# Two PSUM banks re-shared, the masked q copies on ScalarE, and new orders of issue in a fused attention, feed-forward and routing kernel

## What is computed

```python
q = sigmoid(x @ Wq + bq); k = sigmoid(x @ Wk + bk); v = x @ Wv + bv     # per head
sink_in = n / sum((q + e) * (cumsum(k) + e));  src_out = n / sum((k + e) * (cumsum(q) + e))
cons_sink = sum((q + e) * (cumsum(k * src_out) + e)) / n
cons_src  = exp(clip(sum((k + e) * (cumsum(q * sink_in) + e)) / n, -1, 1))
qs = q * sink_in / n;  vs = v * cons_src / cumsum(cons_src) * n
attn = (qs @ cumsum(k^T vs)) * sigmoid(cons_sink) @ Wo + bo
h  = layernorm(x + attn) * g1 + be1
h2 = layernorm(h + gelu(h @ W1 + b1) @ W2 + b2) * g2 + be2              # 256 -> 1024 -> 256
r  = layernorm(x + h2)
e  = argmax(r @ router_w)                                               # one of 8 experts
out = layernorm(r + relu(r @ fc[e])**2 @ pj[e])                         # 256 -> 1024 -> 256
```

## Time and profile before

| | us |
|---|---|
| median of 3 runs | 819.72 (818.33 to 820.4) |
| the profiled execution | 821.92 |
| its span, first to last instruction | 819.8 |
| PE busy in it | 782.9 (95%) |
| DVE busy | 558.9 (68%) |
| POOL busy | 368.1 (45%) |
| ACT busy | 311.6 (38%) |

### The profile page before, as it was taken

The page is one execution under the profiler, slowest core; times in us unless marked ns, Lnnn a source line. Parts: engine busy times, 40 slices in busy tenths (PEclk is TensorE's granted clock), DMA queues, the critical chain, the costliest instruction groups (busy, mean ns, idle before and its releaser), DMA issues.

```text
span 819.8 us, 18747 instructions
## 1 busy us (share of the span) xinstructions
PE 782.9 (95%) x6828; PEld 597.2 (73%) x6828; DVE 558.9 (68%) x1209; ACT 311.6 (38%) x571; POOL 368.1 (45%) x563
## 2 busy tenths in 40 slices
PE   7888999999999999999999999999999999999994
PEld 3455687687777777777867867788987778777762
DVE  7788677799889889888889885574663433433332
ACT  2323413533533543443443434343114444333442
POOL 8210613245556356356257275475334433334434
PEclk9998999999999999999999999999999999999998
DMA  8999999100100100100000000894569898888850
GB/s 242 280 315 305 306 290 285 57 2 2 52 21 8 53 21 7 53 15 15 28 14 14 28 21 19 302 354 168 190 220 400 332 345 314 314 309 296 296 194 13
DMA packets 75193, 133.22 MB, mean 162 GB/s; under 512 B 5725, under 2 KB 54111, under 8 KB 75104
## 3 DMA queue, kind: packets, MB, share of 16 engines
q1 hardware_dynamic: 71936, 123.57, 46.2%
q0 software_dynamic: 3168, 8.46, 2.8%
HBM read 89.35 MB, written 42.93 MB: 161 GB/s over the span
## 4 chain that ended last, share of the span: by engine, by line
PE 79%; DVE 9%; POOL 5%; issue 3%; ACT 1%; DMA 1%; POOLq 0%; DVEq 0%; ACTq 0%
PE bank L958 11%; PE bank L993 11%; PE bank L845 7%; PE bank L857 7%; PE bank L653 4%; PE bank L877 4%; PE bank L1005 4%; PE bank L973 4%; PE bank L888 4%; PE bank L769 3%; PE bank L662 3%; PE bank L807 3%; PE bank L823 3%; DVE sm L1583 2%; POOL rstd L1311 1%
## 5 line engine op out<-in xcount | busy, mean ns | idle before, releaser
L1308 POOL TENSOR_SCALAR vare<-mv 128x1 f32<-128x1 f32 x96 | 24.1, 251 | 202.8 <-DVE mv L1590 198.4
L958 PE MATMUL bank<-xsT,fc 128*128 128x128 f32 x800 | 94.1, 276 | 0.5 <-issue 0.5
L958 PEld LDWEIGHTS bank<-xsT,fc 128*128 128x128 f32 x800 | 91.5, 192 | 3.4 <-issue 3.2
L1583 DVE TENSOR_TENSOR sm<-bank,upto 128x512 f32<-128x512 f32 x128 | 79.3, 681 | 17.3 <-PE bank L769 17.2
L993 PE MATMUL bank<-pj,act 128*128 x336 | 76.2, 380 | 0.5 <-issue 0.5
L845 PE MATMUL bank<-n1T,w1s 128*128 128x256 f32 x256 | 69.9, 396 | 1.8 <-ACT n1T L1113 1.8
L1169 ACT ACTIVATE relu<-bank 128x512 f32<-128x512 f32 x68 | 39.9, 595 | 77.0 <-PE bank L958 49.1
L877 PE MATMUL bank<-n1T,w1s 128*128 128x256 f32 x256 | 67.7, 387 | 1.5 <-ACT hT L1135 0.8
L993 PEld LDWEIGHTS bank<-pj,act 128*128 128x128 f32 x336 | 62.2, 190 | 8.3 <-issue 0.8
L888 PE MATMUL bank<-w2s,hT 128*128 128x256 f32 x256 | 67.3, 385 | 0.0
L857 PE MATMUL bank<-w2s,hT 128*128 128x256 f32 x256 | 66.1, 386 | 0.6 <-ACT hT L1118 0.6
(11 more groups left out here) (267 smaller groups left out, 1672.3 us busy)
## 6 DMA issues: line engine op xcount, KB each, us to landing
routed_rows<-empty SPq DMA_DIRECT2D x64, 520.0 KB, 9.6
fc<-in_fc SPq DMA_DIRECT2D x31, 1024.0 KB, 7.2
up_unit<-in_fc SPq DMA_DIRECT2D x24, 1024.0 KB, 8.1
pj<-in_pj SPq DMA_DIRECT2D x8, 1024.0 KB, 12.4
xrow<-in_fc SPq DMA_DIRECT2D x6, 1024.0 KB, 6.8
x<-in_x SPq DMA_DIRECT2D x8, 512.0 KB, 4.1
xT<-in_xT SPq DMA_DIRECT2D x7, 512.0 KB, 5.1
xs<-routed_rows SPq DMA_DIRECT2D x25, 130.0 KB, 5.7
```

Of the source, the lines that this page charges most:

```text
L958: last = nc.tensor.matmul(h_bank[n][:, chunk(f)], fc[:, at, k, chunk(4 * n + f)], xsT[:, k, :], start=(k == 0), stop=(k == KT - 1))
L1583: nc.vector.tensor_tensor(sm[:, n], BANK4[n][:].rearrange("p (h t) -> p h t", h=4), upto[:].unsqueeze(1).broadcast_to([P, 4, P]), ALU.mult ...
```

## The change

1. **Banks.** Both halves of the feed-forward sum in `po0`, one after the other: `down` of the rest waits until `b_half` has read the half (`r2` to 2), `down` of the next half until `b_add` has read the rest (`r2` to 4). `po1` takes the attention output (columns 0 to 255) and the state update (from column 256).
2. **Waits.** `p_pairs`, `a_share1` and `p_share2` no longer wait for `summed` and `r1`. The update inside `p_mix` waits for `summed` and `r1` of the chunk before, and `p_out` for `summed` of its own chunk.
3. **Copies.** All four `qm` copies of a group are made by ACT in its step `p_share2`; POOL's `p_split` is gone.
4. **First wait.** `t_xb` waits for a semaphore of its own, `bo_in`, in place of all nine transfers behind `tables_in`.
5. **Orders.** All lists are new.

```diff
             load_x(0)
-            for tile, src in ((bo, bo_d), (g1, g1_d), (be1, be1_d), (b2, b2_d), (g2, g2_d), (be2, be2_d)):
+            load_rows_of(bo, bo_d, bo_in)
+            for tile, src in ((g1, g1_d), (be1, be1_d), (b2, b2_d), (g2, g2_d), (be2, be2_d)):
                 load_rows_of(tile, src, tables_in)
...
             def share1(g, half, _):
                 ev["cz"].wait(pe, g, 1)
-                ev["summed"].wait(pe, g - 1, 2)
-                ev["r1"].wait(pe, g - 1, 2)
...
             def pairs(g, half, c):
...
-                ev["summed"].wait(pe, g, c)
-                ev["r1"].wait(pe, g, c)
                 ev["sm"].wait(pe, g, 4 * c)
...
             def mix(g, half, c):
...
                 last.then_inc(S["av"], 1)
+                ev["summed"].wait(pe, g, c)
+                ev["r1"].wait(pe, g, c)
                 for m in range(KT):
                     for j in range(HPT // 2):
                         at = m * P + 32 * j
-                        last = nc.tensor.matmul(ps0[32 * j:32 * j + 32, 32 * m:32 * m + 32],
+                        last = nc.tensor.matmul(po1[32 * j:32 * j + 32, STATE + 32 * m:STATE + 32 * m + 32],
...
             def attn_out(g, half, c):
                 ev["xatc"].wait(pe, g, c + 1)
-                ev["sm"].wait(pe, g, 4 * c + 3)
+                ev["summed"].wait(pe, g, c + 1)
                 for m in range(KT):
-                    last = nc.tensor.matmul(pa[:, 0:D], xat[:, c % 2, m, :], wo[:, m, :],
+                    last = nc.tensor.matmul(po1[:, 0:D], xat[:, c % 2, m, :], wo[:, m, :],
...
             def half_down(g, half, f):
...
                 elif f == 0:
-                    ev["r2"].wait(pe, g - 1, NC // 2)
+                    ev["r2"].wait(pe, g - 1, NC)
...
             def down_ffn(g, half, f):
                 ev["gelu"].wait(pe, g, f + 1)
                 if f == 0:
-                    ev["r2"].wait(pe, g - 1, NC)
-                    if g == 0:
-                        ev["v"].wait(pe, 1, 4)
+                    ev["r2"].wait(pe, g, NC // 2)
                 for c in range(NC // 2, NC):
-                    last = nc.tensor.matmul((po0, po1)[c // 2][:, (c % 2) * D:(c % 2) * D + D],
+                    last = nc.tensor.matmul(po0[:, (c % 2) * D:(c % 2) * D + D],
...
-                    if g == 0 and m == KT - 1:
-                        nc.scalar.activation(qm[:, 1, m], qs[:, m], ACT.Copy, scale=parity[:, 1:2])\
-                            .then_inc(S["qm1"], 1)
+                    nc.scalar.activation(qm[:, 1, m], qs[:, m], ACT.Copy, scale=parity[:, 1:2])\
+                        .then_inc(S["qm1"], 1)
...
-            def split_q(g, half, _):
-                for m in range(KT - 1 if g == 0 else KT):
-                    ev["qp"].wait(pool, g, m + 1)
-                    ev["s"].wait(pool, g - 1, 4 * NC)
-                    apart(pool)
-                    nc.gpsimd.tensor_scalar(qm[:, 1, m], qs[:, m], parity[:, 1:2], None, ALU.mult)\
-                        .then_inc(S["qm1"], 1)
...
             def first_xb(g, half, _):
                 dve.wait_ge(x_in[0], 16)
-                dve.wait_ge(tables_in, 16 * 9)
+                dve.wait_ge(bo_in, 16)
...
             def mix(g, half, c):
                 ev["upd"].wait(dve, g, c + 1)
-                own = ps0[:, 0:KT * 2 * DH].rearrange("p (m n) -> p m n", m=KT)
+                own = po1[:, STATE:STATE + KT * 2 * DH].rearrange("p (m n) -> p m n", m=KT)
...
-            def add_h(g, chunks, bank_of):
+            def add_h(g, chunks):
+                if g == 0:
+                    ev["qp"].wait(dve, 1, KT)
...
```

174 lines of the change are left out of this document (82 added, 92 removed), and 8 rows, old and new, of tables (DVE_LAST, POOL_LAST).

## The result

The change made the kernel slower: 824.66 us median (823.28 to 827.42, 8 runs) against 819.66 (816.02 to 823.71, 8 runs), ratio 1.0061 with an interval of 1.0036 to 1.0085. The forecast was 815.5. (Ratios are of times, this kernel over before; an interval that holds 1 shows no difference.)

A forecast was written before the change was run, and what follows sets the result against it. PE was taken to bound the kernel, busy 782.9 of 819.8 us. Start -4.2, periods +0.6 and end -0.6 gave -4.2 us: 815.5 against the median of 819.72; range, to hold 8 in 10, 812.0 to 821.5.

The forecast's parts named there:

- The comparison place: End of group 2's last a_proj with the first b_up: 107.38 before, forecast 100.6 at full clock, -6.8 us.
- +2.6: Start: loss to half-clock stretches at four thin places, 0.3, 0.3, 1.7 and 0.3 us; bounds 0 and 6.8.
- the walk: The prediction's step-by-step timing of the start in the new order, from differences of start times, at full clock first.
- the start gives it back: Rival: half-clock stretches at all four places of the start cancel its 6.8 us gain; taken at 819, chance 0.23.
- The turn, +0.1 a period: Periods: h_turn's wait for n1T is 0.34 us against 0.26, +0.1 each; +0.6 over seven.
- The copies, zero: Periods: ScalarE's two more copies lie beside a_proj and don't delay the first Gelu; up to 1.33 us a period uncovered.
- The wait of p_out, zero: Periods: p_out's new wait for summed is covered by h_up, 0.86 us; upper bound 0.93 us on 28 places.
- The rival's price of 1.0 us a period: Rival: p_out waits uncovered for summed at chunk 2, 7.0 us in seven periods, 822.5 in all; chance 0.15.
- The shared output bank, zero: Periods: b_half and b_add between downs cost nothing; over 2 us of PE work stands there, DVE needs 0.75.
- The end, -0.6: Last period and LAST: masks later, +0.3; waits of 0.39 at p_out 2 and 0.53 at m_down go; down to -0.9.
- The rule on table loads: Start's Exp load: by the skill's added drain the sum would be 0.8 to 1.4 us worse; drain rival 816.3, chance 0.05.
- full clock: Rival: the start runs without half-clock stretches, giving 812.9 us; chance 0.12.

The follow-up runs named there:

- e2: After with the start's order lists of before, one DVE step moved; early t_xb and ScalarE copies kept: 821.96 us, 1.0016.
- e10: e7 with the start's order lists of before, one DVE step moved as in e2: 817.31 us, 0.9963.
- e5: Before with one change, t_xb waiting for bo alone in its old place: 819.1 us, 0.9981.
- e7: After with c_route 1 moved behind b_up 7 on PE and ScalarE, and GpSimd's d_count 3 behind p_mix 1: 819.88 us, 0.9989.
- e9: e7 with the odd masked copies of groups 1 to 7 back on GpSimd: 821.46 us, 1.0018.
- e6: Before with all four masked copies on ScalarE, without GpSimd's p_split, orders, banks and waits unchanged: 827.21 us, 1.0070.
- e16: e6 with ScalarE's p_share2 (the copies) moved behind the Gelu of b_up 0: 823.06 us, 1.0018.
- e11: e7 with PE's h_up 4 moved from ahead of p_out 2 to its old place ahead of p_mix 2: 820.62 us, 1.0005.
- e15: e11 with DVE's p_state 2 moved back behind a_dots2: 826.02 us, 1.0063.
- e4: After's banks, waits, first wait and ScalarE copies with before's lists, except moves the shared bank forces: 838.41 us, 1.0229.
- e12: e7 with ScalarE's Exp table load ahead of the exponentials of group 0, as in before: 818.8 us, 0.9979.
- e13: e7 with PE's t_shift moved forward in the start, from behind p_out 1 to behind p_out 0: 823.44 us, 1.0033.
- e8: Before with the four LAST lists of after and nothing else: 818.84 us, 0.9982.
- e17: Before with t_xb's own wait (e5) and the four LAST lists of after (e8): 815.86 us, 0.9923.
- e3: After with the four LAST lists of before, b_half 7 placed behind c_sum2 6 1 on DVE: 826.75 us, 1.0072.
- e1: After with ScalarE's c_row 2 moved from behind b_up 6 to behind h_turn 1: 823.7 us, 1.0045.

## Where the prediction was right and where it failed

- **What bounds the kernel.** Right: PE, and what is to be won lies in the start.
- **The start up to 60 us.** Right to 0.6 us: `a_dots2` 34.0 (33.91), `p_share2` 41.8 (41.56), `p_pairs` 1 53.4 (53.68), `t_shift` 59 (60.01). Times in brackets are measured.
- **The start from 60 us on.** Failed, and the largest miss of all. The comparison place was at 106.48, not 100.6 plus 2.6. The term **+2.6** for half clock was sized one stretch at a time; behind `t_shift` there were 13 us of it in one piece, with 11.4 us of PE work, up to 5.7 us where 1.7 was taken. And the walk missed the 1.60 us for `n`. The rival "the start gives it back" was right on the start (its 819 still had a gain elsewhere): by e2 and e10 the new start is 2.6 to 2.7 us slower than the old one with the early `t_xb`, most or all of it clock.
- **The base of the sum.** Failed: gains were read from one execution that was 2.3 us above the median that before had beside after, with its waits at full length. The 3.38 us at `t_xb` gave 1.5 us by itself (e5).
- **The turn, +0.1 a period.** The wait that I priced came as priced: 0.35 us for `n1T` in each period (2.4 us in seven) for the forecast 0.34. What failed is what I left at nothing, and it is the largest miss in the periods: I compared the cover behind the turns and not what stands ahead of them. PE waited for the last Gelu of the rest, 0.81 to 0.97 us, and e7 got 1.0 us back in each of four periods.
- **The copies, zero.** Right in the new order (e9), and mostly for the reason given, that the first Gelu is ahead of them (e6, e16). The price without cover was put at up to 1.33 a period; measured 0.7. The load of Gelu's table behind them was left out.
- **The wait of p_out, zero.** The number was right (0.2 us in after). The reason, `h_up` 4 on PE, was not needed (e11): the walk did not see that `p_state` 2 now stands ahead of `a_dots2` on DVE, which does it by itself (e11 against e15). The rival's price of 1.0 us a period was exact with both gone. In part this was luck.
- **The shared output bank, zero.** Once 0.43 us in after; it can cost 5.3 where `b_half` stands behind the tables (e4).
- **The end, -0.6.** Failed: the last period lost 2.8 us, `LAST` won 0.8 net in this pair. The tables' place on DVE was priced +0.3; a DVE instruction held for 2.1 us came on top, and the Gelu's wait once more. How the 2.8 us divide is not shown.
- **The rule on table loads.** The Trainium skill's page "ScalarE: Activation LUTs", section "What ACT_TABLE_LOAD costs", adds a drain of about 1380 ns to a load. It did not show here. e12 took a load of 1.28 us off the path and `a_comp` came 1.33 us earlier. In e6's rows above the copy ahead of a load ends at 298.45, the load goes from 298.46 to 299.74, and the next activation starts at 299.76, so there is no room for it on either side.
- **The range.** Its lower end was added up twice: "full clock" at 812.9 already has the end at -0.6, so with the end at -0.9 it is 812.6, not 812.0. Nothing hangs on it.

In the terms of the sum: the start was put at -4.2 and gave -0.7 by equal work, the periods were put at +0.6 and gave +1.9, the end was put at -0.6 and gave +2.0. That is 7.3 us of miss; with the 1.9 us of the base it makes the 9.2 us between 815.5 and 824.66.

The slowdown has three parts. The `h_turn` waits cost 4.8 us, 4.0 in the periods and 0.8 in the last one (shown by e7). The new start costs 2.6 us against the old one with the early `t_xb` (shown by e2 and e10), so 1.1 against before, whose `t_xb` costs 1.5 (e5); why the new start gets less clock stays open, as e13 failed to separate it. The rest of the last period costs 2.0 us: by equal work e7's and e10's profiles lose as much there, e8's and e17's, with the old periods, nothing; its cause is read from the trace, not tried. The new `LAST` gives 2.1 us back (e3). Together 5.8 us for the 5.0 measured, as close as timings of different groups allow.

## What to carry to other kernels

When an order changes, follow each engine's queue ahead of every wait, not only what covers the wait behind it: the 0.8 us at `h_turn` came through ScalarE, DVE and GpSimd from a scatter issued too early, as far as the trace tells. Take a gain off the median of several executions, and cost half clock as the whole run of work behind a thin place. And before a large reordering is taken whole, time its independent parts alone: here the two that needed no new banks made a kernel 5.9 us faster than before, and all together made it 5.0 slower.

## What was not expected of the hardware

- GpSimd's `xb` addition (1024 columns, 2.34 us, from 485.92) and a DVE instruction of 16 columns that began 0.02 us later ended together: 2.36 us in place of 0.23. In all thirteen profiles with `p_xb` at its new place in GpSimd's list it took 2.35 to 2.37, in all seven with the old place 0.23 or 0.24. The Trainium skill, "SBUF — State Buffer", section "Who interferes with whom", has a rule for this: DVE and GpSimd share a pair of ports that one instruction holds to its end, and `tensor_scalar` of DVE is among those that can ask for it. The trace agrees as far as it goes: the two end within 0.04 us of each other.
- The granted clock of the start differs between executions of the same code: with the same lists in the start, the clock loss there was 10.2 us in the profile of after, 6.8 in e1's and 13.7 in e3's, some 5 us of time between the last two by the estimate of 0.7 to 0.8. One profile says little of it.
